# Loading the feed-forward weights of the last stage straight into their buffers, and reading them with strides

## What is computed

```python
h = _layernorm(x, axis=-1) * (1 + cb) + sb
gate = einsum('bsh,oh->bso', h, gate_wq * gate_scale[:, None])   # gate_wq: 1792 x 512, int32
up   = einsum('bsh,oh->bso', h, up_wq * up_scale[:, None])       # up_wq:   1792 x 512, int32
x = x + gb * einsum('bsh,oh->bso', silu(gate) * up, down_wq * down_scale[:, None])  # down_wq: 512 x 1792
```

## Time and profile before

| | us |
|---|---|
| median of 3 runs | 1870.27 (1869.86 to 1870.95) |
| span of the profiled execution | 1871.4 |
| PE busy, matmuls | 1819.4 (97% of the span) |
| DVE busy | 1279.4 (68%) |
| ACT busy | 1123.6 (60%) |

### The profile page before, as it was taken

The page is one execution under the profiler, slowest core; times in us unless marked ns, Lnnn a source line. Parts: engine busy times, 40 slices in busy tenths (PEclk is TensorE's granted clock), DMA queues, the critical chain, the costliest instruction groups (busy, mean ns, idle before and its releaser), DMA issues.

```text
span 1871.4 us, 29017 instructions
## 1 busy us (share of the span) xinstructions
PE 1819.4 (97%) x8863; PEld 1516.6 (81%) x8863; DVE 1279.4 (68%) x3032; ACT 1123.6 (60%) x2620; POOL 446.5 (24%) x429
## 2 busy tenths in 40 slices
PE   6898999999999999999999999999999989999999
PEld 4456788888888888888888888888888877888887
DVE  5588677777777677766777777767777786544533
ACT  5564766667667676766666666767676673433331
POOL 2123331231404132332423121240413132010000
PEclk8798999999999999999999999999999999999999
DMA  9005657575766667577767767677776767313010
GB/s 343 2 23 184 193 175 222 170 224 176 203 199 205 201 202 214 174 237 217 220 208 203 217 195 227 183 223 194 213 213 202 209 185 243 121 57 111 25 45 23
DMA packets 239368, 331.25 MB, mean 177 GB/s; under 512 B 26008, under 2 KB 165528, under 8 KB 238880
## 3 DMA queue, kind: packets, MB, share of 16 engines
q1 hardware_dynamic: 238736, 328.93, 58.9%
q10 hardware_dynamic: 528, 1.05, 0.1%
HBM read 200.39 MB, written 129.50 MB: 176 GB/s over the span
## 4 chain that ended last, share of the span: by engine, by line
PE 85%; DVE 5%; ACT 5%; DMA 3%; issue 1%; SPq 1%; DVEq 0%; ACTq 0%
PE ps L1963 25%; PE ps L2029 16%; PE ps L2154 11%; PE ps L2011 10%; PE ps L1996 9%; PE ps L2136 5%; DMA turned_blocks<-tp 2%; PE ps L1170 2%; ACT probs L2252 1%; PE ps L2015 1%; PE ps L1993 1%; PE ps L120 1%; DVE pt L2518 1%; PE ps L1138 1%; DMA pd<-turned_blocks 1%
## 5 line engine op out<-in xcount | busy, mean ns | idle before, releaser
L1963 PE MATMUL ps<-hA,wq 128*128 128x512 f32 x1536 | 385.9, 400 | 0.0
L2029 PE MATMUL ps<-wo,oT 128*128 128x512 f32 x1536 | 367.0, 389 | 3.0 <-issue 1.6
L2494 DVE CUSTOM_DVE_ANT_0 ps<-ps,mask 128x512 f32<-128x512 f32 (+3 forms) x512 | 235.7, 523 | 151.2 <-PE ps L1996 150.7
L2029 PEld LDWEIGHTS ps<-wo,oT 128*128 128x128 f32 x1536 | 288.0, 188 | 62.9 <-issue 1.8
L2271 ACT ACTIVATE pt<-pd 128x1280 fp32r<-128x1280 f32 x128 | 163.0, 1274 | 274.8 <-PE ps L2011 243.0
L1963 PEld LDWEIGHTS ps<-hA,wq 128*128 128x128 f32 x1536 | 279.1, 188 | 56.4 <-issue 0.2
L2252 ACT ACTIVATE probs<-ps,nmax 128x512 f32<-128x512 f32 (+3 forms) x512 | 263.2, 532 | 74.2 <-DVE nmax L2494 74.0
L2260 ACT ACTIVATE probs<-probs,rinv 128x512 f32<-128x512 f32 (+3 forms) x512 | 246.3, 552 | 38.2 <-DVE rinv L2500 38.2
L2011 PE MATMUL ps<-pt,V 128*128 128x512 f32 (+2 forms) x1152 | 252.9, 349 | 11.0 <-DVE pt L2518 10.6
L2011 PEld LDWEIGHTS ps<-pt,V 128*128 128x128 f32 x1152 | 196.2, 190 | 39.7 <-issue 14.6
L1996 PE MATMUL ps<-kT,qT 128*128 128x512 f32 (+2 forms) x1152 | 224.1, 339 | 0.0
(11 more groups left out here) (256 smaller groups left out, 2617.0 us busy)
## 6 DMA issues: line engine op xcount, KB each, us to landing
turned_blocks<-tp SPq DMA_DIRECT2D x128, 640.0 KB, 3.5
pd<-turned_blocks SPq DMA_DIRECT2D x512, 160.0 KB, 3.3
wq_next<-in_L_attn_w_q_dram SPq DMA_DIRECT2D x16, 1024.0 KB, 6.1
wo_in<-in_L_attn_w_o_dram SPq DMA_DIRECT2D x15, 1024.0 KB, 6.9
turned_weights<-hf_chunk SPq DMA_DIRECT2D x168, 64.0 KB, 2.6
wm<-in_L_wmod_dram SPq DMA_DIRECT2D x4, 2048.0 KB, 13.6
turned_values<-tv SPq DMA_DIRECT2D x32, 256.0 KB, 2.8
xh_m<-turned_weights SPq DMA_DIRECT2D x28, 256.0 KB, 3.6
```

The costliest lines, as they stand in the source:

```text
L1963: last = nc.tensor.matmul(ps[:, bank, :], w[i][:, c, cols], hT[k][:, c, b * S:(b + 1) * S], start=(c == 0 and n == 0), stop=(c == DC - 1 a ...
L2029: last = nc.tensor.matmul(ps[:, bank, :], oT[x_][:, b, h, r * P:(r + 1) * P], wo[y_][:, h, :], start=(h == 0 and n == 0), stop=(h == GQ - ...
L2494: nc.vector.tensor_tensor_reduce(out=v, in0=v, in1=mask[:, TB * P - KEYS[i]:], scale=-1.0, scalar=3e38, op0=ALU.add, op1=ALU.min, accum_ou ...
```

## The change

Turned tiles are loaded straight to `ww[j][k]`. The 28 copies on DVE and the 14 on ACT are gone, and so are the landing places. For gate and up tiles `turn_tile` now writes its blocks in the order (b i c): the four chunks stand innermost, and PE picks chunk c by reading every fourth element, 16 bytes apart, as its stationary operand (`stationary`). Down tiles keep their order, and PE reads them in 16 runs of 32 elements as the moving operand (`moving`). The loads get a new order in SP's queue, with waits for the attention's buffers; gate and up tiles of a step are counted by one of four semaphores `ld_wide`, down tiles by `ld_down`. PE waits for `wide_in(j)` in place of a copy.

```diff
-                landing = [xh_m[:, k, :] for k in range(4)] + [xr[:].rearrange("p t i -> p (t i)"), hf_chunk[:]]
-
-                def load_turned(sp, q):
-                    sp.dma_start(landing[q % SLOTS_W], turned_w[q // 3, :, q % 3]).then_inc(ld_w[q % SLOTS_W], 16)
...
+                def wide_in(j):
+
+                    return ld_wide[j % 4], 32 * (j // 4 + 1)
+
+                def load_wide(sp, j):
+                    if j >= 4:
+                        sp.wait_ge(*wide_in(j - 4))
+                    for k in range(2):
+                        sp.dma_start(ww[j][k][:].rearrange("p c i -> p (c i)").bitcast(F32), turned_w[j, :, k]) \
+                            .then_inc(ld_wide[j % 4], 16)
+
+                def load_down(sp, j):
+                    sp.dma_start(ww[j][2][:].bitcast(F32), turned_w[j, :, 2]).then_inc(ld_down, 16)
+
+
+                def stationary(j, k, c):
+                    return ww[j][k][:].rearrange("p c i -> p (c i)").rearrange("p (m c) -> p c m", c=DC)[:, c]
+
+                def moving(j, chunks=slice(0, DC)):
+                    return ww[j][2][:].rearrange("p (a c i) -> p c a i", a=NQD, c=DC)[:, chunks]
...
                                 if not more and u >= 6:
-                                    for q in range(2 * (u - 6), 2 * (u - 6) + 2):
-                                        load_turned(sp, q)
+
+                                    sp.wait_ge(q_full, UNITS * NG)
+                                    sp.wait_ge(wo_split, GQ * NG)
+                                    load_wide(sp, u - 6)
...
                             sp.wait_ge(s["w_kept"], 16 * NQD * TILES + 16)
-                            next_weights(4)
-                            next_weights(5)
+                            sp.wait_ge(k_full, PAIR * NG)
+                            load_wide(sp, 2)
                             store_out(1, 0)
-                            next_weights(6)
-                            next_weights(7)
+                            load_wide(sp, 3)
                             store_out(1, 1)
-                            next_weights(8)
                             store_out(1, 2)
                             store_out(1, 3)
-                            for q in range(9, TILES // 3):
-                                next_weights(q)
+
+
+                            sp.wait_ge(plo_done, UNITS * NG)
+                            sp.wait_ge(o_full, UNITS * NG)
+                            for j in range(4, 8):
+                                load_wide(sp, j)
+                            for j in range(8):
+                                load_down(sp, j)
...
                             if t == 2:
-                                for q in range(TILES // 3, TILES // 3 + 8):
-                                    next_weights(q)
+
+                                sp.wait_ge(w_full, NP * NG)
+                                for j in (8, 9):
+                                    load_wide(sp, j)
...
-                        for q in range(TILES // 3 + 8, TILES):
-                            next_weights(q)
+                        sp.wait_ge(stored, 16 * NT)
+                        for j in range(10, FC):
+                            load_wide(sp, j)
+                        for j in range(8, FC - 1):
+                            load_down(sp, j)
+                        sp.wait_ge(s["dgb"], B)
+                        load_down(sp, FC - 1)
...
-                                    last = nc.tensor.matmul(ps[:, t, :], hd[j][k][:, t * P:(t + 1) * P], ww[j][2][:],
+                                    last = nc.tensor.matmul(ps[:, t, :], hd[j][k][:, t * P:(t + 1) * P], moving(j),
...
-                                pe.wait_ge(*placed(3 * j + 1))
+                                pe.wait_ge(*wide_in(j))
...
-                                        last = nc.tensor.matmul(ps[:, 2 * (j % 2) + k, :], ww[j][k][:, c, :], fT[x_][:, c, :],
+                                        last = nc.tensor.matmul(ps[:, 2 * (j % 2) + k, :], stationary(j, k, c), fT[x_][:, c, :],
...
-                        pe.wait_ge(*placed(TILES - 1))
+                        pe.wait_ge(ld_down, 16 * FC)
...
-                        def place_down(j):
-                            act.wait_ge(*loaded(3 * j + 2))
-                            nc.scalar.activation(ww[j][2][:].rearrange("p (c a i) -> p c a i", a=NQD, c=DC), by_chunks(3 * j + 2),
-                                                 ACT.Copy).then_inc(s["w_scalar"], 1)
...
-                            nc.vector.transpose(out=hf_chunk[:].rearrange("p (b c i) -> p c b i", b=NQD, c=DC),
+                            wide = (step_of(g, i)[1] if isinstance(g, int) else i // 2) < 2
+                            order = "p (b i c) -> p c b i" if wide else "p (b c i) -> p c b i"
+                            nc.vector.transpose(out=hf_chunk[:].rearrange(order, b=NQD, c=DC),
                                                 in_=xr[:].rearrange("p c (b j) -> p c b j", b=NQD)).then_inc(s["w_vector"], 1)
-
-                        def place_wide(j):
-                            for k in range(2):
-                                q = 3 * j + k
-                                dve.wait_ge(*loaded(q))
-                                nc.vector.tensor_copy(ww[j][k][:].rearrange("p c (a i) -> p c a i", a=NQD), by_chunks(q)) \
-                                    .then_inc(s["w_vector"], 1)
```

More of the change, by code:

```diff
@@ L192, in adaln_two_blocks @@
         kv_in, q_in = sem("kv_in"), sem("q_in")
-        ld_w = [sem(f"ld_w{k}") for k in range(6)]
+        ld_tile, ld_down = sem("ld_tile"), sem("ld_down")
+        ld_wide = [sem(f"ld_wide{j}") for j in range(4)]
         ld_xm, ld_at_first = sem("ld_xm"), sem("ld_at_first")
@@ L2164, in last_down @@
                             t = TB - 1
[L2165 removed]
+                            for bank, half, chunks in ((t, slice(0, D // 2), slice(0, DC // 2)), (BANK_Q, slice(D // 2, D), slice(DC // 2, DC))):
                                 for j in range(FC):
                                     for k in range(2):
[L2168 removed]
+                                        last = nc.tensor.matmul(ps[:, bank, half], hd[j][k][:, t * P:(t + 1) * P], moving(j, chunks),
                                                                 start=(j == 0 and k == 0), stop=(j == FC - 1 and k == 1))
```

34 lines of the change are left out of this document (2 added, 32 removed).

## The result

| | before | after |
|---|---|---|
| median of 20 runs each | 1869.76 us (1866.00 to 1881.67) | 1879.86 us (1872.73 to 1885.86) |
| ratio of the times, 95% interval | | 1.0056 [1.0042, 1.0069] |
| span of the profiled execution | 1871.4 us | 1878.1 us |

The changed kernel is slower: by 10.1 us between the medians, by 0.56% as a ratio. The forecast was no change. The range held the time, and the case that came true, slower, had a chance of 0.28.

A forecast was written before the change was run, and what follows sets the result against it. PE's matmul stream was taken as the bound, 226.7 ns apart in the last stage, set by the moving operand. The terms summed 0 + 0 + 0 + 0 + 0, so the forecast was 1870.3 us, range 1867 to 1890.

The forecast's parts named there:

- slower: Outcome case for the whole kernel: a strided weight load past its limit, or a new wait reaching PE; chance 0.28.
- Gate and up weights, every fourth element: 896 strided weight loads in the last stage: 190 ns each, hidden below 227, cost 0; bounds 108 and 432 ns.
- the cover: Gate and up matmuls: a 108 ns weight load hides behind 227 ns, so may grow 2.1 times at no cost.
- the nearest row: DVE's strided read in the trace, 583 ns against 420 plain, 0.64 ns more an element, taken for PE's weight load.
- Down weights in runs: Down matmuls reading 16 runs of 32: cost taken as 0, at most 10 ns each or 4.3 us.
- rival 1: Gate and up: strided weight load exceeds 227 ns; 20 us at 249 ns, 87 or 184 us at three or four times; chance 0.22.
- the sign named for it: Gate and up matmuls over 231 ns apart, the same in every batch, would show the strided load outgrowing 227 ns.
- Copies removed: 28 DVE copies (16.0 us) and 14 ACT copies (8.8 us): PE never waited for one, gain 0, at most 5.1 us.
- PE's five waits: PE's waits from 1529 us to the end, 5.1 us in all, none for a copy; expected to stay the same.
- Loads moved: New load order in SP's queue: every tile lands in time, some 14 us to spare at the least, cost 0.
- Turns: 28 gate and up turns on DVE writing every fourth element: hidden, cost 0; at most 0.33 us each, 9.2 us.
- Same: Outcome case for the whole kernel: no change, 1870.3 us with its own range of 1868 to 1873; chance 0.68.

The follow-up runs named there:

- e8: Ruler on the last stage: gate and up steps with mixed stationary steps, 512 or 256 columns, some inputs in 16 runs; down tiles in various run orders; 1850.83 us.
- e9: Ruler over moving width: gate and up steps with 320 to 512 columns, stationary read plain or with step 2 or 4, down weights plain; 1847.21 us.
- e1: Changed kernel with gate and up weights read as plain neighbouring columns again, down runs kept; 1870.44 us, ratio 1.0009 to the kernel before.
- e2: Changed kernel with down weights read as one run of 512, the strided gate and up read kept; 1876.53 us, ratio 1.0035 to the kernel before.
- e7: Kernel before, copies kept, with only the gate and up copies writing chunks innermost and PE reading every fourth element; 1875.20 us, ratio 1.0028.
- e5: Ruler on the last stage: stationary steps of 1 to 16 elements, some with 256 or 128 columns; down operands in various runs and steps; 1908.8 us.
- e3: Changed kernel with both PE reads plain; direct loads, missing copies and new turns kept; 1868.88 us, ratio 0.9999 to the kernel before.
- e4: Changed kernel with both PE reads plain and DVE's turns in the old order; 1870.49 us, ratio 1.0002 to the kernel before.

## Why the prediction was wrong, though its range held

**What failed.** The step "Gate and up weights, every fourth element". Its sum was 108 + 128 x 0.64 = 190 ns, hidden below 227, cost 0. The load takes 233 ns by itself (e8, e9), 2.16 times the plain one, and the cover is 2.1 times. The price an element is (233 - 108) / 128 = 0.98 ns and not the 0.64 of DVE's strided read the earlier trace rows. That row was no clean price for a step either: the strided instruction also writes 64 results where the plain one writes 4. The cost is 6.6 to 6.8 us (after less e1, e2, e7), where 0 was forecast. The bounds of 108 and 432 ns did hold it.

**The reading of the bound was right, the hard edge was not.** The distance had to be over 227 ns with a load of 233. But the prediction took everything under the cover as free, and it is not: with a step of 3 the load needs 173 ns, and the matmuls of 512 columns still lie 235 ns apart. Had the load taken the 190 ns that I estimated, it would probably have cost about the same. The choice of the nearest row was wrong, and by this second effect a better one within the cover would not have saved the forecast.

**Down weights in runs.** Taken as 0, with 10 ns a matmul or 4.3 us as the upper bound. It is 6.6 ns behind the first tile of each batch (233.3 against 226.7) or 2.8 us to the end (e1). The bound held, and the 0 failed: 6.6 / 15 = 0.44 ns a jump, against the 0.64 of the bound. The argument that a jump at every 32nd element is far from one at each was no reason for 0, since the price doesn't follow the number of jumps: 16 runs cost 6 to 9 ns, 32 or 64 cost 4 to 15 (e5, e8), 256 runs of 2 cost 216, or 0.85 ns a jump and more than the bound, and a step of 2 costs 228. Only the last down part is free. It reads 8 runs, which are free in e5 too, but also only 256 columns, and no run separates the two.

**The sum by the measured terms.** 6.8 (e2) + 2.8 (e1) + 0 (e3) = 9.6 us against 9.4 in the profiled executions and 10.1 between the medians. A single matmul pays 8 ns. The condition of rival 1 is met, a load just past the cover, which was priced at 22 ns each and 20 us, and the sign named for it, over 231 ns in every batch, is what the trace shows. But that sign can't tell rival 1 from the second effect, which no rival named. The range held because it had been stretched for rival 1 and for the runs; that the second effect stayed inside it as well was luck.

**Copies removed, gain 0.** Right. PE's five waits are the same, and e3 has no copies and is not faster. DVE lost 16.0 us of copies and gained 11.3 us of turns; its busy time fell by 1.7 us against 4.7 by this sum, and ACT's by 7.6 against 8.8.

**Loads moved, cost 0.** Right, in their order too: step 4 waited for the last output matmuls, `att_in` came at 1565.87 with a free queue, no tile was late. e3 took the same loads at no cost.

**Turns.** Right that they are hidden (e4), wrong in size: the 42 turns take 40.9 us instead of 29.6, so the 28 changed ones take 0.40 us more each. The upper bound had been 0.33, from a strided read of the same engine; writing every fourth element is dearer than that. The busy times of the kernel after from 850 to 1400 us, against the earlier trace rows:

```profile
850.00:1400.00 550.00, 548.39 (x2728) 470.87 (x2727) 405.32 (x1020) 368.78 (x931) 141.76 (x139) 1.00 0.72 208
```

DVE is at 405 of 550 us, still with room to spare.

**The chances.** "Same" had 0.68, because one row of another engine was allowed to decide a race with a margin of 37 ns, while both bounds of the cost (108 and 432 ns) lay on either side of the threshold. The row was the only one there was, and not a clean one; the margin should have counted for less.

## What to carry to other kernels

A kernel bound by a stream of matmuls pays for the way in which its operands are read, even when no wait shows: look at the distance from start to start, not at busy shares. Keep the stationary operand contiguous where the weight load is near its cover (with 512 columns a step of 4 cost 8 ns of 227, with 256 columns 113 on top of 120), and never put a step on the moving operand, where already every second element doubled the time; runs of 64 or longer were free. And a copy on an engine that nobody waits for is worth nothing to remove: put the layout's price there, as the kernel before did.

## What the runs showed of the hardware

**A threshold in the weight load.** The load's own distance is 108 ns plain (112 in the plain step with 128 columns of e5, where the clock was 1.00), 120 or less with a step of 2, 173 with 3, 233 with 4 and 242 with 8, and at 5, 8 and 16 the records are 302, 331 and 300 ns against 310 with 4: beyond one element in 16 bytes it hardly grows. The rule that the prediction weighed, in the Trainium skill's "SBUF — State Buffer", section on the DMA port swizzle, has that shape: two hits on a 16-byte line for full speed, one is slower. The trace agrees with it for the stationary operand, with 193 ns against 188 for a step of 2. It does not for the moving one, where a step of 2 took 455 ns and runs of 2 took 443. The same note of that section also says that one can stride up to 4 fp32 for free; there the measurement decides against it, since the load with a step of 4 takes 233 ns.

**A small price without an owner.** At 512 columns nearly every departure from contiguous operands that was tried cost something: 7 to 9 ns for a step of 2 or 3 on the stationary side, 4 to 15 for 16 to 64 runs on the moving side; only 4 and 8 runs were free. At 256 and 320 columns a step of 2 cost nothing, nor did 12 runs of 32 at 384, and at 448 and 480 plain matmuls lay 7 and 3 ns above the line through 256 and 512. Plain steps with 512 columns shortly behind a strided one ran at 227.5 to 228.6 ns (steps 4, 7 and 13 of e8), and step 9, right behind a step of 8, at 226.7. Most of the steady distances, 120, 146.7, 173.3, 203.3, 206.7, 216.7, 220, 226.7, 233.3, 236.7 and 240 ns, are whole multiples of 3.33 ns. What sets it stays open; the runs speak against the load's length, a fixed price for each strided matmul, one for the full 512 columns alone, and one that grows with the columns.

The Trainium skill says in "TensorE: Matmul & The Clock Gate", Part 2 on what happens when you issue a matmul, that weights and moving rows come through two read ports of their own, so that loading the next weights takes nothing from the running matmul. For contiguous operands at 512 columns nothing in the trace speaks against it (a load of 108 ns behind 227). With a step of 3 the load needs 173 ns, well inside, and the matmuls lie 235 ns apart; no run here shows whether the ports or something else make the difference.

**The clock fell after a stretch paced by loads.** In e5 steps 9 and 10 have 256 and 128 columns behind loads with a step of 4, steps 11 and 12 the same behind plain loads. Windows of e5, steps 9 to 12 of batch 1; the number ahead of the last two is the granted clock:

```profile
1672.70:1676.20 3.50, 3.50 (x17) 3.50 (x17) 2.05 (x3) 1.32 (x2) 0.00 (x0) 1.00 0.00 0
1676.30:1679.90 3.60, 3.60 (x17) 3.60 (x17) 2.05 (x3) 1.32 (x2) 0.00 (x0) 0.71 0.00 0
1680.00:1683.20 3.20, 3.20 (x16) 3.20 (x16) 1.90 (x7) 1.32 (x2) 0.00 (x0) 0.50 0.00 0
```

During 16 matmuls with 256 columns, 233 ns apart but for the first, the clock was 1.00; over the 16 with 128 columns at the same distance it was 0.71, and in step 11 it was 0.50, the level of 1.2 GHz, although PE is busy throughout by the records. At that level the plain matmuls with 256 columns of step 11 lie 213 ns apart (their median) instead of 120. In the other three batches of e5 the mean over step 11 was 0.50 to 0.57 as well. In e9 steps 10 and 11 have 384 and 320 columns at the same 233 ns, and the clock stayed at 1.00. The kernel after has 512 columns in each 235 ns, and its granted clock from 1547.5 us to the end is 1.00; none of the 9.4 us comes from the clock.
